# Value products of two neighbouring score tiles issued together in every second slot, in the causal half of a gated attention block

## The reference

```python
x = x + tanh(g_xattn) * xattn(layernorm(x), ctx, ctx)       # softmax(q k / sqrt 8) v, 16 heads
def ffn(x, ...):
    q_in = rope(x)
    q, k, v = q_in @ Wq.T + bq, q_in @ Wk.T + bk, x @ Wv.T + bv
    scores = where(causal, q k / sqrt 8, -inf)
    attn_out = (softmax(scores) v) @ out_proj_w.T + out_proj_b
    x1 = layernorm(x + attn_out) * ln1_w + ln1_b
    gates = softmax(x1 @ gate_w.T + gate_b)                  # the two best of 8 experts
    return layernorm(x1 + moe(x1, gates)) * ln2_w + ln2_b
x = x + tanh(g_ffn) * ffn(layernorm(x), ...)
```

## Time and profile before

| | |
|---|---|
| Time, median of three runs | 482.83 us (482.69 to 483.07) |
| Profiled execution, its own time | 483.01 us |
| Its span, first to last instruction | 480.8 us |
| TensorE busy | 420.6 us, 87% |
| VectorE busy | 382.6 us, 80% |
| GpSimd busy | 313.5 us, 65% |
| ScalarE busy | 273.5 us, 57% |
| Mean granted TensorE clock | 0.975 of full speed |

### The profile page before, as it was taken

How to read it: one execution, slowest core, us unless ns; L and a number is a source line. 1 busy time by engine, 2 the same in 40 slices (tenths; PEclk the granted TensorE clock), 3 DMA queues, 4 the chain that set the end, 5 groups by cost and what they waited for, 6 DMA issues and landing times.

```text
span 480.8 us, 18054 instructions
## 1 busy us (share of the span) xinstructions
PE 420.6 (87%) x6804; PEld 265.6 (55%) x6804; DVE 382.6 (80%) x1205; ACT 273.5 (57%) x693; POOL 313.5 (65%) x688
## 2 busy tenths in 40 slices
PE   0378888888888999999999999997899999999983
PEld 0245454544445566666666666664467676767652
DVE  5688999999978878788877787832679899999971
ACT  1136777777676666675666666673354545454440
POOL 5465766767798888878887874220346666666654
PEclk9999999999999999999999999997699999999995
DMA  7855776755533444333344334200000000000000
GB/s 165 195 151 161 194 187 166 184 148 130 134 93 106 110 118 113 95 96 103 104 122 114 94 96 115 66 10 1 1 1 24 11 25 11 24 11 25 12 23 22
DMA packets 88022, 42.78 MB, mean 89 GB/s; under 512 B 15992, under 2 KB 87808, under 8 KB 87936
## 3 DMA queue, kind: packets, MB, share of 16 engines
q1 hardware_dynamic: 77072, 38.87, 30.6%
q10 hardware_dynamic: 10864, 2.76, 2.6%
HBM read 5.68 MB, written 2.10 MB: 16 GB/s over the span
## 4 chain that ended last, share of the span: by engine, by line
PE 37%; DVE 18%; POOL 3%; ACT 2%; issue 2%; ACTq 0%; POOLq 0%; DVEq 0%
PE u_bank L443 8%; DVE z_acc L969 5%; PE s_bank L381 5%; PE s_bank L394 4%; PE s_bank L799 2%; PE u_bank L820 2%; DVE r L617 2%; PE st_bank L799 2%; PE t_bank L373 2%; POOL z_rstd_ L697 2%; PE t_bank L367 2%; PE u_bank L456 2%; PE st_bank L394 2%; DVE z_two L945 1%; DVE z_y L994 1%
## 5 line engine op out<-in xcount | busy, mean ns | idle before, releaser
L636 DVE TENSOR_REDUCE nm<-s_bank 128x4 f32<-128x512 f32 x256 | 171.5, 682 | 37.6 <-PE s_bank L394 34.6
L526 ACT ACTIVATE pt<-st_bank 128x512 f32<-128x512 f32 x256 | 149.1, 601 | 77.2 <-PE u_bank L443 41.1
L394 PE MATMUL s_bank<-qk 64*64 64x128 bf16 (+1 forms) x1536 | 102.5, 221 | 12.2 <-DVE nm L636 7.7
L443 PE MATMUL u_bank<-pt,vaug 128*32 128x128 f32 x2048 | 109.5, 286 | 1.6 <-DVE ao L653 0.3
L394 PE MATMUL st_bank<-qk 64*64 64x128 bf16 (+1 forms) x1588 | 101.7, 218 | 0.0
L394 PEld LDWEIGHTS s_bank<-qk 64*64 64x64 bf16 (+1 forms) x1536 | 72.9, 104 | 36.1 <-issue 18.8
L394 PEld LDWEIGHTS st_bank<-qk 64*64 64x64 bf16 (+1 forms) x1588 | 72.1, 103 | 0.0
L443 PEld LDWEIGHTS u_bank<-pt,vaug 128*32 128x32 f32 x2048 | 40.8, 108 | 27.2 <-issue 3.8
L381 PE MATMUL s_bank<-mqk,idb 64*64 64x256 bf16 x256 | 38.3, 291 | 2.7 <-ACT pt L526 0.8
L884 ACT ACTIVATE z_gated<-s_bank,z_gates 128x128 f32<-128x128 f32 x64 | 18.3, 369 | 35.7 <-PE u_bank L820 35.7
L381 PE MATMUL st_bank<-mkq,idb 64*64 64x256 bf16 x256 | 38.3, 293 | 0.1
(11 more groups left out here) (121 smaller groups left out, 883.0 us busy)
## 6 DMA issues: line engine op xcount, KB each, us to landing
qk<-part SPq DMA_DIRECT2D x221, 128.0 KB, 2.8
x_all<-x SPq DMA_DIRECT2D x16, 128.0 KB, 2.8
qk<-qrow SPq DMA_DIRECT2D x32, 64.0 KB, 2.2
qk<-mts ACTq DMA_DIRECT2D x64, 32.0 KB, 2.5
out<-z_o SPq DMA_DIRECT2D x16, 128.0 KB, 1.8
c_all<-ctx_in SPq DMA_DIRECT2D x14, 128.0 KB, 3.2
ewt<-exp_t SPq DMA_DIRECT2D x1, 512.0 KB
qk<-part ACTq DMA_DIRECT2D x3, 128.0 KB, 2.7
```

Source lines behind the costliest of these rows:

```text
L394: ins = pe.matmul(to[outs, :], fixed[:, outs], moving, start=not masked, stop=True, skip_group_check=masked)
L443: ins = pe.matmul(u_bank[b][32 * j:32 * j + 32, r * P:(r + 1) * P], v, pt[m % 4][:, j, :], start=half == 0, stop=half == 1, skip_group_che ...
L526: act.activation(pt[m % 4][:, :, :].rearrange("k j q -> k (j q)"), st_bank[m % 2][:, :], ACT.Exp).then_inc(ex, 1)
L636: dve.tensor_reduce(nm[q % 2][:, first:first + HEADS], s_bank[n % 2][:, :].rearrange("q (j k) -> q j k", j=HEADS), AX_X, ALU.max, negate=T ...
```

## The change

In the x half nothing changes. In the causal half, slots in which an even tile's A would stand have none, and the next slot has both, the even tile's first. Tiles and matmuls are the same, and so is each tile's place in all other engines' loops. As n - 15 is odd for even n, the slots with a pair are t = 0, 2, 4 and 6.

```diff
@@ in the loop of pe_attention, after scores(tile_n, tile_m)
-                if 0 <= n - AV_LAG < LAST_TILE:
+                if 0 <= n - AV_LAG < GROUPS * TILES:
+                    av(n - AV_LAG)
+                elif (n - AV_LAG) % 2 == 1 and 0 <= n - AV_LAG < LAST_TILE:
+                    av(n - AV_LAG - 1)
                     av(n - AV_LAG)
```

## The result

The changed kernel takes 486.09 us (median of 5 runs, 485.71 to 486.69) against 483.07 us of the kernel before in the same comparison: a ratio of 1.0064, 95% interval 1.0049 to 1.0078, 3.0 us slower by the medians and 3.1 by the ratio. The forecast was 2.4 us slower, and the range holds the time. The profiled execution is the slowest of the five: 486.69 us, with a span of 484.5.

The account below looks back on a forecast made before the run. The prediction took ScalarE and VectorE chains to bound most of each causal unit, TensorE's work only its first stretch and the drain. Units +2.04, groups +0.84 and +0.21, drain -0.70 made +2.4 us: 485.2 us, range 482.4 to 487.9.

Parts of the forecast that it names:

- The stretches: Three parts of a causal unit, 4.47, 3.17 and 2.51 us; TensorE's work counts only in the first, from score block (S) t=0 to t=3.
- 3.17 and 2.51 us: S of t=3 to value projection, then to next S of t=0: chains without value products (A), forecast to stay unchanged.
- The second A: Second block of value products in a pair: forecast to add 0.21 us, taken from the one pair already in the profile.
- the end of the bound at 0.35: Upper end for the cost of a pair's second A: a whole A, 0.35 us.
- the rival of pairs that don't overlap: Second A doesn't overlap the first, accumulating onto the same columns: 0.35 us each, +5.3 us, 488.1 us; 8%.
- The txr limit: Projection after S of t=1 waits for ScalarE's copy of transposed inputs, at least 1.74 us behind that S.
- The unit: Causal period between value projections: from 10.15 to about 10.32 us, +0.17 each, +2.04 us over twelve units.
- The groups: Four-slot groups of the last two units, without projection: +0.21 us each, +0.84 for four, the 2.78 us ScalarE chain staying.
- The drain: From S at 320.06 to the final pair, 8.35 us, where TensorE's work decides: forecast 0.7 us shorter.
- TensorE is the limit everywhere: Faster rival: 63 new pairs save 0.24 us each, 15 us in all, giving 468 us; 6%.
- The ScalarE order is looser: No-change rival: projection doesn't wait for txr, maxima chain starts from the transpose; -0.6 us, 482.3 us; 12%.
- A later maximum of t=6 on VectorE: Worse rival, a new wait: VectorE's maximum falls behind, 0.2 us more in each of 12 units, 487.6 us; 7%.

Follow-up runs that it names:

- Half_t26: Against the kernel before, only tiles with m % 4 = 2 deferred, so pairs stand at t=2 and t=6; 482.79 us, ratio 0.9997.
- half_t04: Against the kernel before, only tiles with m % 4 = 0 deferred, so pairs stand at t=0 and t=4; 486.30 us, ratio 1.0071.
- Before_sc: Kernel before, single A per slot, with ScalarE's causal order changed: txr copy before exp of t=1, copy of maxima moved later; 480.51 us, ratio 0.9953.
- odd_slots: Against the kernel before, odd tiles deferred instead of even, so pairs stand at t=1, 3, 5, 7; 480.50 us, ratio 0.9950.
- after_sc: Changed kernel (pairs at t=0, 2, 4, 6) with txr copied before exp of t=1 and the copy of maxima moved; 484.36 us, ratio 1.0017 against before.

## Why the prediction was right

**The stretches.** The claim that only the work between S of t=0 and S of t=3 decides was right. In the changed kernel 3.17 and 2.51 us stayed to 0.01, although 0.63 us of TensorE's work left them. Half_t26 and half_t04 separate it: second A's at t=2 and t=6 cost nothing, those at t=0 and t=4 cost all. Inside a unit that is the one at t=0, as 3.17 us stay with a pair at t=4; in the groups without projections t=4 opens a group of its own.

**The second A** costs 0.22 us at t=0 (1.62 to 1.84) where 0.21 was taken from a single row. In a pair the next thing starts 0.57 us after the pair (240.84 to 241.41), where a single A has 0.35. So the end of the bound at 0.35, and the rival of pairs that don't overlap, are refuted.

**The txr limit** came out as worked: 1.74 us from S of t=1 to the projection. Moving the copy ahead gave 0.09 us a unit.

**The unit** went from 10.15 to 10.32 us. That is the forecast 0.17, and every unit that no stall touches has it, except the first causal one, which grew by 0.20.

**The groups** grew by the 0.21 forecast where no stall lies in them. Before_sc, in which only ScalarE's order differs, shortens their 2.79 us to 2.70, so it is a ScalarE chain; odd_slots, with a later transpose of the maxima, lengthens it to 2.99.

**The drain** became 0.77 us shorter; the forecast was 0.7.

**Rivals.** "TensorE is the limit everywhere" is refuted three times: two parities with equal merging differ by 5.4 us, half_t26 gains nothing measurable, and the busy share fell while the time rose. The rule of the Trainium skill that a change of tiling mode drains TensorE (TensorEngine Tiling (Array Packing), Key Properties) agrees with the trace so far as the seams go: S follows S after 0.36 us in after_sc (299.78 to 300.14), where A follows S after 0.46. No run here shows that a drain is the cause. The time saved at the seams, seen in the busy time (18.21 us against 19.16), shortens nothing here. It is also smaller than the prediction's 0.24 a pair: at t=1 the transpose of the maxima stands between two S, 0.46 us behind the first (242.22 to 242.68), so that seam is not spared. "The ScalarE order is looser" is refuted by the 1.74 us. A later maximum of t=6 on VectorE does not show: 2.51 stayed.

**What was missing** is the stalls of TensorE inside blocks, 2.2 us in one profile of the changed kernel and 0.7 in the other, in part balanced by the mixture stage, 0.8 and 0.4 us shorter than before, whose matmuls are not changed. The start of the causal half moves as well, though nothing before it was changed: by -0.1 and +0.5 us. With 2.4 us for the terms of the forecast these parts give the 3.7 and 3.2 us by which the two profiled executions are longer than the one of before. The median's 3.0 lies between the forecast and these sums; which share each part has in it is not shown. That the forecast missed by only 0.6 us owes something to these parts having opposite signs.

## What to carry to other kernels

Merging work of one kind can spare time on its engine (here 0.14 us a pair), but the spared time counts only where the engine's own work sets the pace; first cut the loop's period into stretches that end with a wait and stretches that don't. Work that is deferred should move out of the stretch without waits and into one with a wait: the same merge shifted by one slot turned 3.0 us of loss into 2.4 of gain. After each such gain look for what the removed work had covered, here ScalarE's copy of u and then VectorE's read of a bank.

## What the runs showed of the hardware

TensorE can stall inside a block of matmuls for 0.1 to 1.1 us with no semaphore wait in the profile ("issue"). The merged orders have more of it: none or 0.1 us in all in the two kernels with a single A in each slot, 0.6 to 2.7 us in all in the profiles with pairs. The places are not all chance: four profiles with pairs at t=0 have a small stall between 291 and 293 and another between 301 and 304. The stalls keep time with the instruction queue q8, which brings a transfer of 16 KB about every 5 us. In the ten profiles with stalls each of the 31 of 0.1 us and more ends 1.3 to 2.4 us after such a transfer has landed, and the thirteen longest, 0.36 us and more, end 1.3 to 1.5 us after. For the stall at 253.6 the transfer ran from 252.07 to 253.51 and the matmuls go on at 254.94; the transfer before it had started 7.0 us earlier. That speaks for late instruction delivery. It is only argued from those times: the profile does not say whose instructions q8 brings, and no run changed the amount of code.

How long the granted clock stays at half (0.50, the 1.2 GHz level) behind the causal half differs too: 13.7 us in the profile of before, 10.2 in both of the changed kernel, 3.4 in that of half_t04. Ahead of the fall TensorE is mostly idle, busy 1.1 of the 2.6 us behind the last pair's start in before. From the start of the last pair to the end the four profiles take 152.4, 151.6 and 152.1, and 150.8 us. So the less time at half clock, the shorter this part; no run varied the clock alone, and 151.6 against 152.1 at the same 10.2 us shows that something else moves it too.
